# k and v brought to token rows by VectorE block turns and SBUF transfers in a gated delta rule layer (Trainium2, one core)

## What is computed

```python
q, k, v, z = jnp.split(qkvz, [DK, 2 * DK, 2 * DK + DV], axis=-1)
...
mixed = lax.conv_general_dilated(mixed, conv_w, (1,), [(K_CONV - 1, 0)], ...)
...
q = _l2norm(q) * DK ** (-0.5)
k = _l2norm(k)
...
def step(Sstate, xs):
    q_t, k_t, v_t, g_t, b_t = xs
    Sstate = Sstate * jnp.exp(g_t)[..., None, None]
    kv = jnp.einsum('bhk,bhkv->bhv', k_t, Sstate)
    delta = (v_t - kv) * b_t[..., None]
    Sstate = Sstate + k_t[..., :, None] * delta[..., None, :]
    o_t = jnp.einsum('bhk,bhkv->bhv', q_t, Sstate)
    return (Sstate, o_t)
...
var = jnp.mean(o * o, -1, keepdims=True)
o = o * lax.rsqrt(var + EPS) * norm_weight * jax.nn.sigmoid(z)
return o.reshape(Bsz, Sl, VDIM) @ w_out.T
```

## Time and profile before

| | us |
|---|---|
| median of 3 runs | 3640.7 |
| lowest and highest | 3633.98, 3648.48 |
| the profiled execution | 3642.89 |
| its span, first to last instruction | 3641.1 |

### The profile page before, as it was taken

The page is one execution under the profiler, slowest core; times in us unless marked ns, Lnnn a source line. Parts: engine busy times, 40 slices in busy tenths (PEclk is TensorE's granted clock), DMA queues, the critical chain, the costliest instruction groups (busy, mean ns, idle before and its releaser), DMA issues. The chain is left out here.

```text
span 3641.1 us, 118760 instructions
## 1 busy us (share of the span) xinstructions
PE 3372.2 (93%) x51264; PEld 2286.7 (63%) x51264; DVE 2288.9 (63%) x5697; ACT 1788.2 (49%) x3338; POOL 1089.7 (30%) x904
## 2 busy tenths in 40 slices
PE   4489999999999999999999999999999999969998
PEld 2256666666666666666666666666666666645554
DVE  5456666666666666666666666666666666635555
ACT  2245555555555555555555555555555555523333
POOL 1043333333333333333333333333333333300000
PEclk7689999999999999999999999999999999979999
DMA  2233233323333333333332233333332333210000
GB/s 76 65 85 82 82 84 87 83 71 83 85 83 84 87 87 86 86 82 81 85 86 76 77 84 86 85 83 86 87 85 78 84 86 87 63 59 18 23 24 18
DMA packets 572727, 274.83 MB, mean 75 GB/s; under 512 B 475696, under 2 KB 521136, under 8 KB 563888
## 3 DMA queue, kind: packets, MB, share of 16 engines
q1 hardware_dynamic: 572208, 267.25, 27.2%
HBM read 190.02 MB, written 35.13 MB: 62 GB/s over the span
## 5 line engine op out<-in xcount | busy, mean ns | idle before, releaser
L1144 PE MATMUL bank<-xT,w_sb 128*128 128x512 f32 x2048 | 1002.6, 618 | 25.7 <-DMA w_sb<-in_w_qkvz 24.7
L681 POOL TENSOR_TENSOR kq<-kq,products 128x510 f32<-128x510 f32 (+2 forms) x384 | 442.3, 1159 | 892.6 <-ACT products L768 738.4
L1144 PEld LDWEIGHTS bank<-xT,w_sb 128*128 128x128 f32 x2048 | 354.5, 190 | 338.3 <-issue 282.7
L818 ACT COPY delta<-bank 128x256 f32<-128x256 f32 x256 | 95.3, 372 | 639.3 <-PE bank L1227 639.3
L950 DVE SCALAR_TENSOR_TENSOR kq<-bank,cw,kq 128x510 f32<-128x510 f32 (+2 forms) x384 | 285.9, 745 | 101.9 <-ACT kq L762 92.8
L669 POOL TENSOR_TENSOR dec_a<-gcrow,gccol 128x1024 f32<-128x1024 f32 x64 | 121.7, 1901 | 614.0 <-DVE p_t L996 323.5
L950 DVE SCALAR_TENSOR_TENSOR v_c<-bank,cw,v_c 128x510 f32<-128x510 f32 (+2 forms) x384 | 285.8, 744 | 15.2 <-ACT v_c L762 6.2
L1028 DVE TENSOR_TENSOR acc<-acc,bank 128x512 f32<-128x512 f32 x128 | 88.1, 688 | 316.7 <-PE bank L1266 316.7
L1171 PE MATMUL bank<-kq 64*64 64x128 f32 x4096 | 278.5, 275 | 1.7 <-DVE p_t L996 1.7
L1171 PEld LDWEIGHTS bank<-kq 64*64 64x64 f32 x4096 | 217.4, 132 | 76.4 <-issue 71.2
L1266 PE MATMUL bank<-wo,u_sq 128*128 128x256 f32 x1024 | 259.3, 397 | 3.4 <-DVE u_sq L1021 3.4
(11 more groups left out here) (137 smaller groups left out, 6259.7 us busy)
## 6 DMA issues: line engine op xcount, KB each, us to landing
w_sb<-in_w_qkvz SPq DMA_DIRECT2D x64, 1024.0 KB, 6.6
gcrow<-gcrow_d SPq DMA_DIRECT2D x128, 256.0 KB, 4.3
xT<-xT_d SPq DMA_DIRECT2D x64, 512.0 KB, 3.4
k_old<-kq SPq DMA_DIRECT2D x64, 512.0 KB, 3.0
wo<-in_w_out SPq DMA_DIRECT2D x64, 256.0 KB, 6.9
gcrow<-in_x SPq DMA_DIRECT2D x16, 512.0 KB, 3.9
x_un<-eye_un SPq DMA_DIRECT2D x64, 128.0 KB, 2.8
a_d<-a_mat SPq DMA_DIRECT2D x512, 16.0 KB, 1.7
```

The costliest lines, as they stand in the source:

```text
L681: ins = nc.gpsimd.tensor_tensor(t[:, :, d:SEQ], t[:, :, d:SEQ], prod[:, :, 0:SEQ - d], ALU.add)
L1144: ins = nc.tensor.matmul(bank[:, :], w_sb[:, h, s * P:(s + 1) * P], xT[:, h, :], start=(h == 0), stop=(h == HT - 1))
```

## The change

1. Token rows. k_tokens and v_tokens go. VectorE transposes blocks of 32x32 (turn_k into k_tok, turn_v into v_x; two instructions of 128x512 each), and eight DMAs per tensor, SBUF to SBUF, put the blocks of 32 partitions in their places (k_turned into k_f, v_turned into v_f). squares, scale_k and scale_v read k_f and v_f.
2. Whole rows. a_d, z_d and x_d hold whole 64x64 tiles, with one row of padding. units_out, x_back and z_back move whole tiles (`whole`, rows of 64 numbers, two DMAs of 1024 rows), units_in, x_out and z_out only the diagonal blocks (`diagonal`, rows of 16 numbers, two DMAs of 1024 rows). What lies outside the diagonal stays zero; it is written once at the end of the first stage. z_low and its four DMAs go; z_t has two buffers.
3. 48-column merges. join16_inner reads a_mat[.., 0:48] and columns of z_t, join16_outer x_row[.., 0:48], in place of 64 columns.
4. Squares. epsilon_q goes. square_q scales by 0.064, and VectorE adds the result to the squares of the output (add_squares); sum_squares starts its bank.
5. Order. All five turn functions are written anew. TensorE does the join and solve(0) for s[2] at the period's end and the rest of the solution for s[3]; projections stand between the chunks' products; project(0) is the first of a step. SP sends v_turned, units_out, load_gates and so on in a new order; SP's load_xw waits for project(6) of the step before.

```diff
-        a_d, z_d, x_d = (scratch(n, [UNITS, B, B]) for n in ("a_d", "z_d", "x_d"))
+        a_d, z_d, x_d = (scratch(n, [2, G * MAT]) for n in ("a_d", "z_d", "x_d"))
+
+        def whole(t, h):
+
+            return t[h].rearrange("(g x) -> g x", x=MAT)[:, 0:C * C].rearrange("g (i c) -> i g c", c=C)
+
+        def diagonal(t, h):
+
+            return t[h].rearrange("(u x) -> u x", x=MAT * B // C)[:, 0:B * C].rearrange("u (i c) -> u i c", c=C)[:, :, 0:B]
...
                     def units_out(m):
                         for h in range(2):
-                            for k in range(4):
-                                u, r = (4 * h + k) * G, D * h + B * k
-                                sp.dma_start(a_d[u:u + G].rearrange("g i j -> i g j"),
-                                             a_mat[m.par][r:r + B, :, B * k:B * k + B]).then_inc(a_d_out, 16)
+                            sp.dma_start(whole(a_d, h), a_mat[m.par][D * h:D * h + D, :, :]) \
+                                .then_inc(a_d_out, 16)
...
                     def z_out(m):
-                        sp.dma_start(z_d, t_un[:, :, :]).then_inc(z_d_out, 16)
+                        for h in range(2):
+                            sp.dma_start(diagonal(z_d, h), t_un[D * h:D * h + D, :, :]) \
+                                .then_inc(z_d_out, 16)
...
+                            sp.dma_start(z_t[m.par][D * h:D * h + D, :, :], whole(z_d, h)).then_inc(z_in, 16)
...
+                    def k_turned(m):
+                        for h in range(2):
+                            for f in range(2):
+                                for t in range(2):
+                                    r, q = D * h + W2 * t, D * h + W2 * f
+                                    sp.dma_start(k_f[r:r + W2, :, W2 * f:W2 * f + W2], k_tok[q:q + W2, :, W2 * t:W2 * t + W2]) \
+                                        .then_inc(k_f_in, 16)
...
-                    def tokens(src, a, bank):
-                        gate_small()
-                        for i in range(GP):
-                            for h in range(2):
-                                half = slice(D * h, D * h + D)
-                                ins = nc.tensor.matmul(bank[half, i * C:(i + 1) * C], src[half, a, i * C:(i + 1) * C],
-                                                       eye64[half, :], start=True, stop=True)
-                        return ins
...
-                                ins = nc.tensor.matmul(banks[5][half, g * W2:(g + 1) * W2], a_mat[m.par][half, g, :],
-                                                       z_low[half, g, :], start=True, stop=True)
+                                ins = nc.tensor.matmul(banks[5][D * h:D * h + 3 * B, g * W2:(g + 1) * W2], a_mat[m.par][half, g, 0:3 * B],
+                                                       z_t[m.par][half, g, :].rearrange("p (k e c) -> p e k c", k=2, c=B)[:, 1, :, :], start=True, stop=True)
...
-                    def epsilon_q(m, a, bank):
-                        nc.tensor.matmul(bank[:, :], ones[:, 1, :], q_sq[:, a, :], start=True, stop=False)
-
...
```

More of the change, by code:

```diff
@@ L95, in gated_delta_sandwich @@
         kt = [sb(f"kt{i}", [P, G, C]) for i in range(2)]
-        z_t = sb("z_t", [P, G, C])
+        z_t = [sb(f"z_t{i}", [P, G, C]) for i in range(2)]
         k_tok = sb("k_tok", [P, G, C])
@@ new lines, in turn @@
+                        if s[1]:
+                            wait_for(pe, conv_done[4], s[1], 1)
+                            project(s[1], 3, banks[1])
+                        if s[3]:
+                            wait_for(pe, rhs_done[1], s[3], 1)
+                            solve(s[3], 1)
+                        if s[1]:
+                            project(s[1], 5, banks[2])
+                        if s[3]:
+                            wait_for(pe, delta_done[1], s[3], 1)
+                            advance(s[3], 1)
+                            wait_for(pe, qg_done[1], s[3], 1)
+                            output(s[3], 1)
+                            wait_for(pe, state_done[1], s[3], 1)
+                            key_state(s[3], 2)
@@ new lines, in turn @@
+                        if s[3]:
+                            wait_for(pe, sq_added[1], s[3], 1)
+                            sum_squares(s[3], 1, banks[2])
+                            wait_for(pe, mats_done[3], s[3], 1, back=-2)
+                            wait_for(pe, sq_added[0], s[3], 1)
+                            sum_squares(s[3], 0, banks[3])
+                        if s[2]:
+                            wait_for(pe, z_in, s[2], 32)
+                            join16_inner(s[2])
+                        if s[0]:
+                            wait_for(pe, conv_done[0], s[0], 1)
+                            wait_for(pe, tap_done[0], s[0], 1)
+                            project(s[0], 2, banks[0])
```

646 lines of the change are left out of this document (316 added, 330 removed).

## The result

| | before | after |
|---|---|---|
| runs, us | 3634.0 to 3648.5 (4) | 3704.4, 3709.0, 3718.1 |
| profiled execution, us | 3642.9 | 3709.0 |
| its span, us | 3641.1 | 3707.2 |
| mean granted clock | 0.974 | 0.933 |
| TensorE busy | 93% | 84% |

The prediction was 3397 us, with a range that ended at 3640. It had the wrong sign.

The account below looks back on a forecast made before the run. TensorE's work in a row was taken to bound the kernel before; after, VectorE's loop (42.3 us) and the queue loop (42.9) gave a period of 43.3. 659.3 + 8 + 63 x 43.3 = 3395, executed 3397 us, range 3215 to 3640.

Parts of the forecast that it names:

- TensorE's own work: TensorE's work in one period: 47.33 us before, 39.5 after the removals, 40.1 with handoffs of 0.6.
- VectorE's price: Work added on VectorE: turns at 0.70 us each, and 4 us a period of locks with GpSimd (bounds 0 and 8.4).
- VectorE's loop: VectorE from output(3) to new_state(0), then TensorE from output(0) to output(3): 38.3 us, 42.3 with locks (38.3 to 46.7).
- Packets: DMA engines: 13950 more packets a step at 15 ns, 13 us more engine time a period, share 65%.
- the chain: SP's queue from load_xw through x and z out and back: TensorE waits 2.8 us at join16_inner, loop 42.9 us.
- z_in comes 17.0 us after projection 6: Arrival of z behind load_xw and the x and z transfers: 17.0 us, where TensorE reaches join16_inner after 14.2.
- The other half of the ring: Loop from projection 6 through SP's queue and join16_inner to the next projection 6; its part from join16_inner on: 25.9 us.
- the sign that was set for it: In the trace, TensorE's wait at join16_inner for the DMA of z_t should be 2 to 3 us a period.
- The start: Outside the periods: 3 us for zeros written at the first stage's end, 5 us for draining a fuller fourth stage.
- The queue chain sets the pace: Rival, slower: x and z packets at 27.7 ns, join16_inner waits 9.3 us, period 49.4, 3781 us; chance 0.12.

Follow-up runs that it names:

- the run with small additions: GpSimd's six tap additions a step cut from 512 columns to 16, against the kernel with x_out and z_out ahead of load_xw (3515 us): 3457 us, ratio 0.949.

## Where the prediction went wrong

**TensorE's own work: right within 2%.** 40.1 us were forecast with the handoffs of 0.6: 14.2 from projection 6 to join16_inner and 25.9 on. Where z is hardly waited for, the first stretch is 17.0 us, of which 2.7 idle and 0.25 in the wait, so 14.1 of work, a little of it at half clock; at full clock the second is 27.2 with 1.1 idle, so 26.1, where 25.3 of work were forecast.

**VectorE's price: right in sum.** The turns took 0.685 us. The excess of the five groups over their free durations is 15 x 0.114 + 3 x 0.49 + 2 x 0.27 + 2 x 0.26 + 2 x 0.07 = 4.4 us a period; 4 were forecast. By the rule of the Trainium skill ("SBUF — State Buffer", Who interferes with whom) every such operation can be held for a whole one of GpSimd's; the run with small additions agrees for the subtractions, 306 to 207 ns, for decay_state, 690 to 421, and for scale_v, 889 to 688. But VectorE's loop did not set the pace: without its two additions of squares, and with the work back on TensorE, the period grew.

**Packets: the price was right, the chain was not.** 898,112 more packets are 14,033 a step (forecast 13,950), and (51.5% x 3707.2 - 27.2% x 3641.1) x 16 / 898,112 = 16.4 ns each (forecast 15). The run with few k and v transfers gives the price of 128 bytes alone: 458,752 packets less took the share from 51.5% to 42.1%, which is 12.3 ns each, near the 10.9 of 64 bytes in the earlier trace rows. The Trainium skill ("DMA: Bandwidth & Descriptors", Specifications) has rows under 512 bytes read, modified and written; if they are, it made 128 bytes little dearer than 64.

The step that failed is "z_in comes 17.0 us after projection 6": 20.2 in the period shown, 18.8 on average. The sum of engine time was not too small: 20.23 us at a share of 0.84 are 17.0, of which 1.8 belong to v, so 15.2 where 16.0 were forecast. The sum took the engines as busy without a break from projection 6 on. But x and z had to go out, land and come back in series, with SP held 5.47 us in z_out's issues and z_back issued only after all that stands ahead of it in SP's order, 12.0 us after projection 6; in the lulls of that chain the engines had little to do. (z_out had landed 0.9 us or more before every z_back from 600 to 3000 us, so it was SP's turn that z_back waited for, not that landing.)

**The other half of the ring: 25.9 forecast, 29.2 measured.** This is the larger error, 3.3 us, and for half of it there was no term. 1.6 us are the clock behind the wait: 3.5 us at half speed. I had the earlier trace rows with a clock of 1.00 and kept it, although I forecast a wait of 2.8 us that had not been there. TensorE's idle time in this half is 1.5 us, 0.75 for VectorE and 0.7 without a releaser, where 0.6 were forecast for handoffs; the last 0.8 are its work, 26.1 against 25.3.

**Stalls without a releaser** were in no term either: 2.0 us a period, 1.3 of them between projection 6 and join16_inner. There, in the changed kernel, they fall into time in which z is not yet in; once its wait is gone, they are the next thing on the path. They also hid the error from the sign that was set for it: TensorE came to join16_inner later than forecast by about as much as z did (2.2 and 1.8 us), so that the wait of 2.5 us a period stood within the 2 to 3 that the forecast wanted to see, in a period 4.7 us too long.

**The start** was forecast at 8 us and cost 22.

**The rival.** "The queue chain sets the pace" was the right mechanism, at 0.12. Its condition was wrong: I let it decide from a wait of 7.1 us at join16_inner; 2.5 were enough, because I priced a wait as its own length only, with nothing behind it, and had no term for what delays TensorE on its way there. Its reason, packets of 27.7 ns, was wrong too: they cost 16.4.

## To carry to other kernels

Where a transfer lies on a ring with TensorE, follow it issue by issue: what stands ahead of it in the queue, how long the issuing engine is held, and each round trip; the stage's mean share (0.60 here) says nothing. Issue what is ready early ahead of the large load that is only released late. And price a new wait on TensorE with what comes behind it, here 1.6 us lost to the slower clock for 2.5 us of wait.

## What the runs showed of the hardware

- Waits on TensorE of 3.0 us on average (52, up to 5.7) were followed by 3.5 us a period at the lower clock level (1.2 of 2.4 GHz); with matmuls that nobody reads in the wait, the granted clock was 0.99 of full on average.
- Two issues of one line on SP took 5.47 us behind load_xw and x_out, and 1.32 with only x_out ahead of them.
- In the stretch where x and z go out, land and come back, the DMA engines had lulls (shares of 0.46 and 0.17) while SP still had transfers to issue; with x and z ahead of the large load there were none.
- A packet of 128 bytes took 12.3 ns of one DMA engine (by the run that leaves 458,752 of them out), one of 64 bytes 10.9 in the earlier trace rows.
- TensorE stalled by 1.2 to 4.9 us with nothing to wait for, in the changed kernel and its variants and never in the kernel before. In the changed kernel, from 400 to 2900 us, the stalls of over 0.8 us whose end goes with an instruction packet came to 72 us, and to 17 when the weights were spared in the same order. The cause is not shown.
- A fifth less of DMA share (0.60 to 0.49) taken outside the ring gave 0.4%; one load of 1 MB a step taken out of the ring gave 4.7%.
